# Second layer of an AdaLN/FFN kernel: the e4m3 rounding without its masking step, a shorter scale chain, and the last expert tile's w2 split moved ahead

## The chip, the cores and the metric

The kernel runs on one core of one Trainium2 chip. The time is the device time of one execution in microseconds (us). The engines are TensorE (PE, its weight loads PEld), VectorE (DVE), ScalarE (ACT), GpSimd (POOL) and SyncE (SP). All times on a timeline are us from the start of the profiled span.

## The reference

The input x is 4 x 256 x 256. Two layers follow, each `x = x + ffn(cond(x))`.

- `cond` is a bidirectional recurrence over the 256 rows: forward and backward decaying sums of exp(k) and exp(k)*v, their ratio, times sigmoid(x).
- Layer 1's `ffn` is an attention block (16 heads, 4 key heads) and then a mixture of 8 experts, top 2 of 8 for each row: `silu(h @ w1[e]) * (h @ w3[e]) @ w2[e]`, 256 to 896 to 256 wide.
- Layer 2's `ffn` is quantised. Rows are scaled by their largest absolute value over 448 and rounded to e4m3 (three bits of mantissa), the weights likewise:

```
def _reorder_quantize_x(x, idx):
    scale = jnp.max(jnp.abs(x)) / GLOBAL_DIV
    xr = (x / scale)[:, idx]
    scale_x = jnp.max(jnp.abs(xr), axis=1, keepdims=True) / FP8_MAX
    qx = _fp8(xr / scale_x)
    return (qx, scale_x, scale)
...
g = _qlinear(qx, sx, sc, w_gate, up_reorder_index, out_idx=down_reorder_index)
u = _qlinear(qx, sx, sc, w_up, up_reorder_index, out_idx=down_reorder_index)
t = jax.nn.silu(g) * u
qt, st, sct = _reorder_quantize_x(t, down_reorder_index)
y = _qlinear(qt, st, sct, w_down, down_reorder_index)
```

The inner width is 704.

## The kernel before, in words

The kernel is written engine by engine; each engine has its own list of instructions in a fixed order, and semaphores order them against one another. `link(ins)` lets DVE wait until `ins` has finished before the next instruction may start; without it short instructions overlap in the pipeline.

**The expert loop** (PE L653, ACT L998, DVE L1547). The 1024 rows, each for two experts, are sorted by expert into 23 tiles of 128 rows (MT = 23, tiles 0 to 22). Products with large weights are made with a value split into a high and a low float16 part. For tile n:

- PE makes the up products in two parts (`up`, 512 and 384 columns of w1 and w3), then, one tile behind, the down product (`down`, L635), which waits for the low parts of inner rows and w2 (`inner_low`, `w2lo_done`) and until ACT has copied the output before from the same bank (`y_copied`).
- ACT, in this order: Silu of the first part (L1007), a copy of the next tile's transposed rows, `w2_high` (L971: the high part of the expert's w2, 1792 columns, which waits until the down product of tile n-2 has read the buffer), `inner_high` of the first part, Silu of the second part (L1019), `inner_high` of the second part, the copy of tile n-1's output out of PSUM (L1028) and its write to memory (L1030).
- DVE: `silu(n, 0)` (multiplies the first part, L1519), a piece of side work for layer 2, `silu(n, 1)`, `inner_low(n, 0)` (L1533), `w2_low` (L1526), `inner_low(n, 1)`, another piece of side work.
- At the end of the loop come two folds, in which layer 2's gate and up weights, already multiplied by their scales on POOL, are split into high and low parts: `fold_high` on ACT (L994, behind tiles 20 and 21, since n runs one ahead of the output) and `fold_low` on DVE (L1545, behind tiles 21 and 22).

**Between the layers.** When all outputs are in memory, POOL gathers the two expert outputs of each row (L1846), in five groups of 1, 1, 2, 2 and 2 of the eight 128-row tiles (`GROUPS`). PE waits for the first combined group and then runs fillers (`keep_clock`, L404, products of zeros).

**The second layer**, per group g and tile i:

- DVE `combine` (L1571) adds the two weighted outputs to the residual; ACT takes the Sigmoid (`input_gate`, L1039); DVE `mix_input` multiplies by the ratio (L1595) and calls `scale_of_rows`: the peak of each row (L1579), the output scale peak/448 (L1580), its reciprocal (L1581), and that times 2^20 (L1582). ACT `scaled_input` makes two scaled copies: the value (L1055) and the value times 2^20 (L1056).
- DVE `round_input` calls `nearest_e4m3`: L1586 keeps the exponent bits of the raised copy and sets one bit of the mantissa, which gives the constant 1.5 times a power of two; L1587 adds it (or a least value) to the scaled value, which rounds it; L1588 subtracts it again.
- PE transposes, makes the gate and up products (L686). ACT takes the Silu of the gate (`gate_of_tile`, L1066). DVE `inner_rows` multiplies by the up product (L1614) and calls `scale_of_rows`. ACT `scaled_inner` makes the two copies (L1073, L1074), DVE `round_inner` rounds, PE transposes (L710), ACT copies (L1080), PE makes the down product (L720), DVE `output_rows` scales it (L1631), POOL adds the residual (L1852) and SP writes it.
- DVE's order is written out by hand (L1634 to L1663). In the steady part it is inner_rows(i), round_inner(i-1), output_rows(i-3). ACT's is scaled_inner(j+1), gate_of_tile(j+2), copy_qxT(j+3), copy_qtT(j) (L1107). Before tile 2 ACT loads the table of Silu by a one-column Silu (L1097), behind the Sigmoids of the last groups.

The rounding as it stands:

```
link(V.tensor_scalar(g.bitcast(I32), raised.bitcast(I32), 0x7F800000, 0x00400000, ALU.bitwise_and, ALU.bitwise_or))
link(V.scalar_tensor_tensor(v, g, FP8_LEAST * MAGIC, v, ALU.max, ALU.add))
return V.scalar_tensor_tensor(dst, g, FP8_LEAST * MAGIC, v, ALU.max, ALU.subtract, reverse1=True)
```

Of the kernel before, what the change touches and what calls it, by code (L numbers as in the profile page):

```python
# [7 lines left out]
I32 = mybir.dt.int32  # L8
U32 = mybir.dt.uint32
ALU = mybir.AluOpType  # L10
# [33 lines left out]
FP8_LEAST = 2.0 ** -6  # L44
GROUPS = ((0, 1), (1, 1), (2, 2), (4, 2), (6, 2))
# [20 lines left out]
def build(nc, t, out):  # L66
    ctx = ExitStack()
    with ctx:
# [86 lines left out]
        xval, xraised, xgrid = (cut(breg, 2 * NT * D + k * 2 * D, 2 * D).rearrange("p (i n) -> p i n", i=2) for k in range(3))  # L155

        gate0, gate1, tval0, tval1, tsc0, tsc1, tra0, tra1, tgrid = (cut(areg, 8832 + k * INTER, INTER) for k in range(9))
# [602 lines left out]
        def _(act):  # L760
# [237 lines left out]
            for n in range(MT + 1):  # L998
# [14 lines left out]
                if n < MT:  # L1013
                    w2_high(n, parity)
                    inner_high(n, parity, 0)
                    act.wait_ge(s["upb_done"], n + 1)
# [3 lines left out]
                    if n + SLOTS_UP < MT:  # L1020
                        load_up(act, n + SLOTS_UP)
                    inner_high(n, parity, 1)
# [8 lines left out]
                if n in (20, 21):  # L1031
                    fold_high(n - 20)
# [14 lines left out]
            def scaled_input(g):  # L1047
# [5 lines left out]
                for k in range(count):  # L1053
                    i = first + k
                    nc.scalar.activation(xval[:, k, :], xmix[:, i, :], ACT.Copy, scale=rs[:, 4, i:i + 1])  # L1055
                    last = nc.scalar.activation(xraised[:, k, :], xmix[:, i, :], ACT.Copy, scale=rs[:, 5, i:i + 1])  # L1056
# [12 lines left out]
            def scaled_inner(i):  # L1069
# [4 lines left out]
                nc.scalar.activation(traised[i % 2], tvals[i % 2], ACT.Copy, scale=rs[:, 9, i:i + 1]).then_inc(s["scaled_ready"], 1)  # L1074
# [43 lines left out]
        def _(dve):  # L1118
# [428 lines left out]
            for n in range(MT):  # L1547
# [5 lines left out]
                w2_low(n, n % 2)  # L1553
# [3 lines left out]
                if n >= MT - 2:  # L1557
                    fold_low(n - MT + 2)
# [17 lines left out]
            def scale_of_rows(at, value, i, n, done):  # L1576

                peak, out, inverse, raised = (rs[:, k, i:i + n] for k in at)
                link(V.tensor_reduce(out=peak, in_=value, axis=AX.X, op=ALU.max, apply_absolute_value=True))  # L1579
                link(V.tensor_scalar(out, peak, 1.0 / FP8_MAX, None, ALU.mult))  # L1580
                link(V.reciprocal(inverse, out))  # L1581
                V.tensor_scalar(raised, inverse, 2.0 ** 20, None, ALU.mult).then_inc(done, 1)  # L1582

            def nearest_e4m3(dst, v, raised, g):

                link(V.tensor_scalar(g.bitcast(I32), raised.bitcast(I32), 0x7F800000, 0x00400000, ALU.bitwise_and, ALU.bitwise_or))  # L1586
                link(V.scalar_tensor_tensor(v, g, FP8_LEAST * MAGIC, v, ALU.max, ALU.add))  # L1587
# [291 lines left out]
```

## Time and profile before

| | |
|---|---|
| median of 3 runs | 626.72 us (625.84 to 627.07) |
| the profiled execution | 625.02 us, span 623.2 us |
| mean granted TensorE clock | 0.961 |
| busy: PE, PEld, DVE, ACT, POOL | 495.9, 406.4, 506.2, 361.1, 241.2 us |
| stages | to about 20: loading; to 170 and 310: recurrence, attention; to 540: experts; from 545.8 to 617: second layer |

A timeline row reads: start, duration, engine, line, operation, what is written from what with partitions x elements, how many, and in brackets the idle time before it and what ended it. "issue" there is time in which the engine waited for nothing that the profile shows. The clock is a share of 2.4 GHz; it has two levels, 1.00 and 0.50 (1.2 GHz).

### The profile page before, as it was taken

The page shows a single profiled execution, that of the slowest core. Times are in us where ns is not written, and L with a number is a line of the kernel's source. Part 1 is how long each engine was busy: PE and PEld are TensorE (multiplying, and loading weights), DVE is VectorE, ACT ScalarE, POOL GpSimd, SP SyncE. Part 2 cuts the span into 40 slices and gives each one's busy share as a digit, 9 for nine tenths or more (in the row PEclk, how much of TensorE's full clock was granted, in tenths as well). Part 3 has the DMA queues.
Part 4 walks back from the last instruction along what each step waited for, and adds up shares of the span by engine and source line. Part 5 has one row for each costly group of instructions (what it writes and reads, how often), then busy time and mean ns, then how long its engine had stood idle before and what let it go on. Part 6 is the DMA issues. An engine that isn't in the chain of part 4 may idle for free.

```text
span 623.2 us, 10889 instructions
## 1 busy us (share of the span) xinstructions
PE 495.9 (80%) x3862; PEld 406.4 (65%) x3862; DVE 506.2 (81%) x981; ACT 361.1 (58%) x762; POOL 241.2 (39%) x204
## 2 busy tenths in 40 slices
PE   2011298599999999999748999999999999475774
PEld 1000143278888878888618999999999999332542
DVE  4999878688888888987354979989999899489993
ACT  3336235777787778876307457565555556356671
POOL 3244014744444445541436079642514420170011
PEclk9999999989999999999859999999999999888897
DMA  8300004050000000000149799889888753130001
GB/s 267 135 1 1 0 1 135 0 178 2 1 2 2 1 2 9 19 9 2 58 157 357 259 331 281 273 267 257 300 290 271 274 130 119 34 103 17 9 25 36
DMA packets 36530, 71.87 MB, mean 115 GB/s; under 512 B 5275, under 2 KB 21915, under 8 KB 36219
## 3 DMA queue, kind: packets, MB, share of 16 engines
q10 hardware_dynamic: 15280, 40.77, 19.6%
q1 hardware_dynamic: 18123, 22.26, 10.6%
q0 software_dynamic: 3072, 8.14, 5.2%
q8 instruction: 31, 0.51, 0.4%
q14 instruction: 24, 0.20, 0.1%
HBM read 66.03 MB, written 5.12 MB: 114 GB/s over the span
## 4 chain that ended last, share of the span: by engine, by line
PE 55%; DVE 27%; issue 7%; ACT 5%; DMA 3%; POOL 1%; SPq 1%; DVEq 0%; ACTq 0%; POOLq 0%; PEldq 0%
PE pw L437 9%; PE pb L437 9%; PE pt L631 6%; PE pb L631 6%; PE sc L478 6%; PE sc L631 6%; PE po L437 5%; PE pt L489 3%; DVE areg L1181 2%; DVE areg L1167 2%; DVE areg L1165 2%; DVE rs L1579 2%; DMA wreg<-in_L_ffn_w 1%; DVE breg L1238 1%; DVE areg L1614 1%
## 5 line engine op out<-in xcount | busy, mean ns | idle before, releaser
L1730 POOL TENSOR_TENSOR breg<-breg,con 128x512 f32<-128x512 f32 x32 | 40.7, 1272 | 81.4 <-ACT breg L864 81.4
L437 PE MATMUL pb<-areg,wreg 128*128 128x512 f16 x240 | 58.4, 379 | 2.1 <-ACT breg L864 1.9
L437 PE MATMUL pw<-areg 128*128 128x256 f16 x406 | 56.5, 273 | 2.7 <-DVE areg L1533 2.7
L872 ACT ACTIVATE breg<-breg,mx 128x128 f32<-128x128 f32 (+1 forms) x128 | 56.5, 444 | 2.0 <-DVE mx L1289 2.0
L478 PE MATMUL sc<-areg,breg 128*128 128x128 f32 (+1 forms) x256 | 48.6, 334 | 6.7 <-DVE mx L1289 5.5
L631 PE MATMUL pb<-areg,wreg 128*128 128x128 f32 x448 | 52.7, 275 | 0.6 <-ACT areg L965 0.6
L985 ACT CAST areg<-areg 128x512 f16<-128x512 f32 (+1 forms) x46 | 25.9, 563 | 46.8 <-DVE areg L1519 43.6
L631 PEld LDWEIGHTS pb<-areg,wreg 128*128 128x128 f32 x448 | 51.3, 192 | 0.9 <-issue 0.8
L631 PE MATMUL pt<-areg,wreg 128*128 128x128 f32 x424 | 49.9, 275 | 1.3 <-DMA wreg<-in_L_ffn_w 1.3
L631 PEld LDWEIGHTS pt<-areg,wreg 128*128 128x128 f32 x424 | 48.5, 192 | 1.5 <-DMA wreg<-in_L_ffn_w 1.4
L631 PE MATMUL sc<-areg,wreg 128*128 128x128 f32 x416 | 48.9, 275 | 0.0
L478 PEld LDWEIGHTS sc<-areg,breg 128*128 128x128 f32 x256 | 38.7, 193 | 14.3 <-issue 4.6
L631 PEld LDWEIGHTS sc<-areg,wreg 128*128 128x128 f32 x416 | 47.6, 192 | 0.1
L1725 POOL TENSOR_TENSOR breg<-breg 128x512 f32<-128x512 f32 x32 | 44.5, 1390 | 4.5
L1772 POOL DMA_INDIRECT areg<-h_dram,row_ids x23 | 28.1, 1222 | 45.3 <-PE po L618 33.2
L881 ACT CAST breg<-pt 128x768 f16<-128x768 f32 x32 | 25.5, 798 | 34.4 <-PE pt L489 34.3
L437 PEld LDWEIGHTS pw<-areg 128*128 128x128 f16 x406 | 39.5, 98 | 7.3 <-DVE areg L1533 3.0
L977 ACT ACTIVATE areg<-wreg 128x1792 f16 x23 | 39.2, 1704 | 3.0 <-issue 2.7
L1289 DVE CUSTOM_DVE_ANT_0 breg<-sc,con 128x128 f32<-128x128 f32 (+1 forms) x128 | 38.0, 353 | 2.4 <-PE pt L489 1.6
L437 PEld LDWEIGHTS pb<-areg,wreg 128*128 128x128 f16 x240 | 22.3, 98 | 26.3 <-ACT breg L864 3.4
L1238 DVE TENSOR_TENSOR breg<-pb,con 128x512 f32<-128x512 f32 x40 | 27.5, 687 | 13.4 <-PE pb L437 10.9
L414 PE MATMUL sc<-con,areg 128*128 128x128 f32 x16 | 4.5, 434 | 42.3 <-DVE areg L1184 42.3
(250 smaller groups left out, 1286.4 us busy)
## 6 DMA issues: line engine op xcount, KB each, us to landing
wreg<-in_L_ffn_w ACTq DMA_DIRECT2D x40, 896.0 KB, 8.1
wreg<-in_L_ffn_w SPq DMA_DIRECT2D x14, 896.0 KB, 8.3
ys_dram<-areg ACTq DMA_DIRECT2D x23, 128.0 KB
wreg<-in_L_ffn_wq SPq DMA_DIRECT2D x1, 2048.0 KB, 8.9
wreg<-in_L_ffn_wo SPq DMA_DIRECT2D x1, 2048.0 KB, 8.2
areg<-in_fside_BxSxS ACTq DMA_DIRECT2D x4, 256.0 KB, 5.4
x_in<-in_x SPq DMA_DIRECT2D x4, 256.0 KB, 3.9
h_dram<-areg SPq DMA_DIRECT2D x8, 128.0 KB, 1.7
```

The lines of the kernel that those rows point to most:

```text
L437: last = nc.tensor.matmul(bank, w(a), m(b), start=first and k == 0, stop=final and k == 2)
L478: last = nc.tensor.matmul(sc2[:, b, o:o + w], qr[:, buf, b * S + qb * P:b * S + (qb + 1) * P], kT[:, kv, pair * PAIR + b * S:pair * PAIR + ...
L631: last = nc.tensor.matmul(bank[:, j * P:(j + 1) * P], up_w[n % SLOTS_UP][:, m, c, at:at + P], xsT[:, parity, c * P:(c + 1) * P], start=c = ...
L872: last = nc.scalar.activation(pr[:, parity, b, o:o + w], pr[:, parity, b, o:o + w], ACT.Exp, bias=mx[:, parity, k:k + 1], scale=-1.0, accu ...
L881: nc.scalar.copy(pT[:, parity, 0], pt2[:, :, 0:BLK]).then_inc(s["pThi_done"], 1)
L977: nc.scalar.activation(w2s[parity][0].rearrange("p c n -> p (c n)"), wreg[:, bass.ds((e % RING) * WDOWN, WDOWN)], ACT.Copy, scale=WS).then ...
L985: nc.scalar.copy(hhT[parity][:, 0, lo // P:hi // P, :], inner[:, lo:hi].rearrange("p (c n) -> p c n", n=P))\
L1238: V.tensor_tensor(t1[:, parity, :].rearrange("p (b n) -> p b n", b=2), bank[:, :].rearrange("p (b n) -> p b n", b=2), rope_cos.rearrange(" ...
L1289: last = V.tensor_tensor_reduce(out=pr[:, parity, b, o:o + w], in0=sc2[:, b, o:o + w], in1=mask[:, o:o + w], scale=-SCALE, scalar=3e38, op ...
L1725: G.tensor_tensor(dst, t1[:, parity, :], t2[:, parity, :], ALU.add).then_inc(s["radd_done"], 1)
L1730: G.tensor_tensor(t2[:, parity, :].rearrange("p (b n) -> p b n", b=2), t2[:, parity, :].rearrange("p (b n) -> p b n", b=2), rope_sin.rearr ...
L1772: G.indirect_dma_start(out=xs[n % 4], out_offset=None, in_=h2_dram[:, :], in_offset=bass.IndirectOffsetOnAxis(ap=row_ids[:, n:n + 1], axis ...
```

## The change

- `nearest_e4m3` loses its first instruction. ACT makes the raised value with Abs instead of Copy, and the row's factor becomes 448/peak times (2^20 - 2^10) instead of times 2^20. This value itself, not 1.5 times a power of two, is added and subtracted.
- `scale_of_rows` takes the reciprocal of the peak first (a linked step); the inverse, the raised inverse and the output scale then follow without a link between them. For the input groups the output scale, which was an instruction of its own in `mix_input`, becomes the last of these four.
- The last tile's `w2_high` and `w2_low` go ahead, behind the work of tile 21; on the last tile ACT takes `inner_high` of the first part behind the second Silu. The two `fold_high` move one tile later (the second behind the last output), both `fold_low` behind the last tile.

```diff
+RAISE = 2.0 ** 20 - 2.0 ** 10
...
-                if n < MT:
+                if n < MT - 1:
                     w2_high(n, parity)
                     inner_high(n, parity, 0)
+                if n < MT:
                     act.wait_ge(s["upb_done"], n + 1)
                     if n >= 1:
                         act.wait_ge(s["inner_low"], 2 * n)
                     nc.scalar.activation(inner[:, FA:FF], up_pair(n, 1)[:, 0, 0:FB], ACT.Silu).then_inc(s["silu_b_done"], 1)
                     if n + SLOTS_UP < MT:
                         load_up(act, n + SLOTS_UP)
+                    if n == MT - 1:
+                        inner_high(n, parity, 0)
                     inner_high(n, parity, 1)
...
-                if n in (20, 21):
-                    fold_high(n - 20)
+                if n == MT - 2:
+                    w2_high(MT - 1, 1 - parity)
+                if n >= MT - 1:
+                    fold_high(n - MT + 1)
...
-                    last = nc.scalar.activation(xraised[:, k, :], xmix[:, i, :], ACT.Copy, scale=rs[:, 5, i:i + 1])
+                    last = nc.scalar.activation(xraised[:, k, :], xmix[:, i, :], ACT.Abs, scale=rs[:, 5, i:i + 1])
...
-                nc.scalar.activation(traised[i % 2], tvals[i % 2], ACT.Copy, scale=rs[:, 9, i:i + 1]).then_inc(s["scaled_ready"], 1)
+                nc.scalar.activation(traised[i % 2], tvals[i % 2], ACT.Abs, scale=rs[:, 9, i:i + 1]).then_inc(s["scaled_ready"], 1)
...
-                w2_low(n, n % 2)
+                if n < MT - 1:
+                    w2_low(n, n % 2)
                 inner_low(n, n % 2, 1)
                 if n in beside_b:
                     beside_b[n]()
-                if n >= MT - 2:
-                    fold_low(n - MT + 2)
+                if n == MT - 2:
+                    w2_low(MT - 1, (MT - 1) % 2)
+            for m in range(2):
+                fold_low(m)
...
-            def scale_of_rows(at, value, i, n, done):
+            def scale_of_rows(at, value, i, n, done, step):
 
-                peak, out, inverse, raised = (rs[:, k, i:i + n] for k in at)
+                peak, turned, out, inverse, raised = (rs[:, k, i:i + n] for k in at)
                 link(V.tensor_reduce(out=peak, in_=value, axis=AX.X, op=ALU.max, apply_absolute_value=True))
-                link(V.tensor_scalar(out, peak, 1.0 / FP8_MAX, None, ALU.mult))
-                link(V.reciprocal(inverse, out))
-                V.tensor_scalar(raised, inverse, 2.0 ** 20, None, ALU.mult).then_inc(done, 1)
+                link(V.reciprocal(turned, peak))
+                V.tensor_scalar(inverse, turned, FP8_MAX, None, ALU.mult)
+                V.tensor_scalar(raised, turned, FP8_MAX * RAISE, None, ALU.mult).then_inc(done, 1)
+                return V.tensor_scalar(out, peak, step, None, ALU.mult)
 
-            def nearest_e4m3(dst, v, raised, g):
+            def nearest_e4m3(dst, v, raised):
 
-                link(V.tensor_scalar(g.bitcast(I32), raised.bitcast(I32), 0x7F800000, 0x00400000, ALU.bitwise_and, ALU.bitwise_or))
-                link(V.scalar_tensor_tensor(v, g, FP8_LEAST * MAGIC, v, ALU.max, ALU.add))
-                return V.scalar_tensor_tensor(dst, g, FP8_LEAST * MAGIC, v, ALU.max, ALU.subtract, reverse1=True)
+                link(V.scalar_tensor_tensor(v, raised, FP8_LEAST * MAGIC, v, ALU.max, ALU.add))
+                return V.scalar_tensor_tensor(dst, raised, FP8_LEAST * MAGIC, v, ALU.max, ALU.subtract, reverse1=True)
...
-                scale_of_rows((2, 0, 4, 5), value, first, count, s["xinv_ready"])
-                V.tensor_scalar(rs[:, 3, first:first + count], rs[:, 0, first:first + count], 1.0 / WS, None, ALU.mult).then_inc(s["xout_ready"], 1)
+                scale_of_rows((2, 0, 3, 4, 5), value, first, count, s["xinv_ready"], 1.0 / (FP8_MAX * WS)).then_inc(s["xout_ready"], 1)
...
-                scale_of_rows((6, 7, 8, 9), tval, i, 1, s["inv_ready"])
+                scale_of_rows((6, 1, 7, 8, 9), tval, i, 1, s["inv_ready"], 1.0 / FP8_MAX)
```

The buffers of the masked value (`xgrid`, `tgrid`) are dropped with it.

## Rows read from the trace of the kernel before

**Rows 1.** DVE's timeline, tail of the expert loop: start, us, engine, line, operation.
```profile
529.37 1.62 DVE L1545 SCALAR_TENSOR_TENSOR x_in<-breg,x_in 128x1408 f16<-128x1408 f32 x1
530.91 0.69 DVE L1519 TENSOR_TENSOR areg<-areg,pt 128x512 f32<-128x512 f32 x1
...
533.74 2.02 DVE L1526 SCALAR_TENSOR_TENSOR areg<-wreg,areg 128x1792 f16<-128x1792 f16 x1
535.68 0.55 DVE L1533 TENSOR_TENSOR areg<-areg 128x384 f16<-128x384 f32 x1
...
545.78 1.01 DVE L1571 SCALAR_TENSOR_TENSOR x<-areg,rt,x 128x256 f32<-128x256 f32 x2 [8.01 <-DMA areg<-ys_dram,sloti]
```

**Rows 2.** PE's timeline, the same stretch.
```profile
528.22 2.84 PE L631 MATMUL pb<-areg,wreg 128*128 128x128 f32 x24
...
536.28 2.47 PE L437 MATMUL pw<-areg 128*128 128x256 f16 x21 [2.71 <-DVE areg L1533]
```

**Rows 3.** ACT's timeline, the same stretch.
```profile
527.31 0.33 ACTq L1030 DMA_DIRECT2D ys_dram<-areg  x1
527.69 1.38 ACT L994 ACTIVATE w_up<-breg 128x1408 f16<-128x1408 f32 x1 [0.41 <-ACT areg L1028]
...
529.70 1.71 ACT L977 ACTIVATE areg<-wreg 128x1792 f16 x1
...
533.94 0.39 ACT L1028 ACTIVATE areg<-pw 128x256 f32<-128x256 f32 x1
```

**Rows 4.** Busy time and granted clock in windows: PE, PEld, DVE, ACT, POOL, PEclk, DMA.
```profile
589.00:609.00 20.00, 14.15 (x113) 9.55 (x110) 19.18 (x37) 13.01 (x17) 2.19 (x3) 1.00 0.07 23
...
571.80:575.20 3.40, 3.40 (x14) 1.80 (x12) 2.85 (x8) 0.85 (x1) 0.00 (x0) 0.50 0.00 0
```

**Rows 5.** DVE's timeline, second layer, tiles 2 and 5.
```profile
575.68 0.95 DVE L1614 SCALAR_TENSOR_TENSOR areg<-pb,rs,areg 128x704 f32<-128x704 f32 x1 [0.86 <-issue]
...
594.13 0.94 DVE L1614 SCALAR_TENSOR_TENSOR areg<-pb,rs,areg 128x704 f32<-128x704 f32 x1
...
596.02 0.15 DVE L1580 TENSOR_SCALAR rs<-rs 128x1 f32<-128x1 f32 x1
...
596.49 0.53 DVE L1586 TENSOR_SCALAR areg<-areg 128x704 int32<-128x704 int32 x1
597.05 0.89 DVE L1587 SCALAR_TENSOR_TENSOR areg<-areg 128x704 f32<-128x704 f32 x1
...
599.18 0.94 DVE L1614 SCALAR_TENSOR_TENSOR areg<-pb,rs,areg 128x704 f32<-128x704 f32 x1
```

**Rows 6.** DVE's groups of line 1586 by shape: busy us, mean ns, idle before.
```profile
L1586 DVE TENSOR_SCALAR areg<-areg 128x704 int32<-128x704 int32 x8 | 4.3, 533 | 0.6 <-PE pt L710 0.6
...
L1586 DVE TENSOR_SCALAR breg<-breg 128x512 int32<-128x512 int32 x3 | 1.3, 418 | 0.0
...
L1586 DVE TENSOR_SCALAR breg<-breg 128x256 int32<-128x256 int32 x2 | 0.6, 294 | 0.9 <-ACT breg L1056 0.9
```

**Rows 7.** ACT's timeline, second layer, ahead of tile 2 and at tile 5.
```profile
569.42 1.28 ACT L1097 ACT_TABLE_LOAD   x1
...
596.60 0.88 ACT L1073 ACTIVATE areg<-areg,rs 128x704 f32<-128x704 f32 x1 [1.04 <-DVE rs L1582]
...
598.16 0.83 ACT L1066 ACTIVATE areg<-sc,rs 128x704 f32<-128x704 f32 x1
```

**Rows 8.** PE's timeline, second layer: products of tile 2, of tile 7, and the tail.
```profile
571.34 2.11 PE L686 MATMUL sc<-x_in,areg 128*128 128x352 f16 x8 [0.46 <-ACT areg L1045]
573.24 2.34 PE L686 MATMUL pb<-w_up,areg 128*128 128x352 f16 x8
...
601.91 1.36 PE L686 MATMUL pb<-w_up,areg 128*128 128x352 f16 x8
...
609.04 0.82 PE L710 MATMUL pt<-identb,areg 128*88 128x128 f16 x8 [3.10 <-DVE areg L1588]
609.65 1.92 PE L720 MATMUL pw<-areg 88*128 88x256 f16 x8
```

More of the change, by code:

```diff
@@ L154, in build @@
         xsig, xmix = (cut(breg, k * NT * D, NT * D).rearrange("p (i n) -> p i n", i=NT) for k in range(2))
-        xval, xraised, xgrid = (cut(breg, 2 * NT * D + k * 2 * D, 2 * D).rearrange("p (i n) -> p i n", i=2) for k in range(3))
-        gate0, gate1, tval0, tval1, tsc0, tsc1, tra0, tra1, tgrid = (cut(areg, 8832 + k * INTER, INTER) for k in range(9))
+        xval, xraised = (cut(breg, 2 * NT * D + k * 2 * D, 2 * D).rearrange("p (i n) -> p i n", i=2) for k in range(2))
+        gate0, gate1, tval0, tval1, tsc0, tsc1, tra0, tra1 = (cut(areg, 8832 + k * INTER, INTER) for k in range(8))
         tscaled, traised = (tsc0, tsc1), (tra0, tra1)
@@ L1603, in round_input @@
                     dve.wait_ge(s["qxT_done"], first + count - 4)
-                nearest_e4m3(qx[:, first // 2 % 2, first % 2:first % 2 + count, :], xval[:, 0:count, :], xraised[:, 0:count, :],
-                             xgrid[:, 0:count, :]).then_inc(s["qx_ready"], 1)
+                nearest_e4m3(qx[:, first // 2 % 2, first % 2:first % 2 + count, :], xval[:, 0:count, :], xraised[:, 0:count, :]).then_inc(s["qx_ready"], 1)
             def inner_rows(i):
@@ L1623, in round_inner @@
                     dve.wait_ge(s["qtT_done"], i)
-                nearest_e4m3(qt[:, :], tscaled[i % 2], traised[i % 2], tgrid).then_inc(s["qt_ready"], 1)
+                nearest_e4m3(qt[:, :], tscaled[i % 2], traised[i % 2]).then_inc(s["qt_ready"], 1)
             def output_rows(i):
```

## The prediction

> **What bounds the kernel now.** I read the busy time by stage first, then for the two stretches that the change touches the timelines of VectorE (DVE), ScalarE (ACT) and TensorE (PE), then the groups of DVE instructions. Two stretches matter.
>
> The tail of the expert loop. On tile 22, the last, DVE multiplies the first half at 530.91 and must then wait for ACT's second Silu before it can multiply the second; behind that come the low split of w2 at 533.74, which holds the engine for two us, and the low half of the inner rows at 535.68 [rows 1]. PE had finished the last up products at 531.06 (528.22 + 2.84) and starts the last down product at 536.28, after 2.71 us of waiting for that last DVE instruction [rows 2]. ACT is no better: after the first Silu of tile 22 it makes the high w2 split (529.70, 1.71 us), so that its second Silu comes late, though its input was there at 531.06 [rows 2, 3]. Everything after the last down product is a chain of a copy, a write, a gather and then DVE at 545.78 [rows 1]; DVE idles 8 us for it, so a us gained at 536.28 is a us of the end.
>
> The second layer, from 545.8 on. In the stretch of tiles 5 to 7 DVE is busy 19.18 of 20 us, PE 14.15, ACT 13.01 [rows 4]. A tile takes DVE 5.05 us (594.13 to 599.18) [rows 5].
>
> **The change, part by part.**
>
> (1) The tail. Removed from tile 22: ACT's w2 split between the two Silus and DVE's low split between the two low halves. They go behind tile 21, in the place of one fold. The steps after:
> - ACT: the write of tile 20 is issued at 527.31 and takes 0.33; then the register load and the split of 1.71, from about 527.97 to 529.67. It replaces the fold of 1.38 there (527.69), so the first Silu of tile 22 starts 0.6 later, at about 529.55 [rows 3]. This costs nothing: DVE comes to it later still.
> - DVE: the low split (two us) takes the place of the fold of 1.62 at 529.37; it waits for ACT and runs 529.72 to 531.65, so the first multiplication of tile 22 goes from 530.91 to 531.65.
> - ACT's second Silu starts at 531.10 (PE's 531.06), ends 531.6. DVE's second multiplication follows at 532.25, the two high halves on ACT at 532.3 and 532.8, the low halves on DVE at 532.9 and 533.5, ending 534.05.
> - The last down product also waits until ACT has copied the output of tile 21 out of the same bank: 533.94 + 0.39 = 534.33 [rows 3]. That ends last: start 534.38. Gain 536.28 - 534.38 = 1.90 us.
> - The folds. ACT issues a write, folds (1.38) from 534.74 to 536.1, copies tile 22 at 536.9, and folds again 537.7 to 539.1; DVE's two folds of 1.62 end at 537.8 and 540.8. The gather brings DVE's next work at 545.78 - 1.90 = 543.88, so 3.1 us of cover is left. Without it the second fold would cost its 1.62. The table load behind the second fold ends before 540.5, under the same cover. The queues of SP and POOL get nothing new and nothing of theirs is passed; the write of tile 22 is issued before the second fold.
>
> (2) The masking instruction on line 1586 goes: eight of 704 columns, three of 512, two of 256 [rows 6]. From start to start they hold DVE 0.56 (596.49 to 597.05 [rows 5]) for 704 columns; for the others I add the 0.03 of hand-over that this shows over the mean: 0.45 and 0.32. Sum 4.48 + 1.35 + 0.64 = 6.5 us of DVE.
>
> (3) The scale chain. Before, three short instructions, two of them linked: 596.02 to 596.49, 0.47 [rows 5], which I split as two linked steps of 0.20 and a last one of 0.07. After, one linked step and three of 0.07, 0.41: 0.06 falls. For the five input groups, where the output scale was a fourth instruction already (0.54), 0.13 falls. ACT's scale is ready 0.13 earlier: one linked step of 0.20 less, one of 0.07 more. So 8 x 0.06 + 5 x 0.13 = 1.1 us of DVE.
>
> (4) Abs for Copy on ACT: no row has Abs. The nearest rows are Copy with the scale (0.88) and Silu with the scale, as wide (0.83): I take 0.88, no change; with 0.83 each tile would gain 0.05. The other end is a table load in front of it, 1.28; that is a rival below [rows 7]. The two Copies and the Silus and Sigmoids alternate already with no load for Copy, which is why I stay at the near end.
>
> What of (2) and (3) reaches the end? Not all, and this is where I chose. Times are of the trace before, without the 1.90.
> - To the first instruction of tile 2 (575.68 [rows 5]) DVE loses 0.64 + 0.45 + 2 x 0.56 and 4 x 0.13 + 2 x 0.06, together 2.85, and it had waited 0.86 there: it would be ready at 571.97. But it waits for PE's up products, which end at 575.58 (573.24 + 2.34), and these stand behind a table load on ACT (569.42), which follows the last combine [rows 7, 8]. Up to that combine only 0.64 + 0.56 + 3 x 0.13 + 2 x 0.06 = 1.71 falls, some 0.05 of it taken back by PE at tile 1. So tile 2 is 1.66 earlier.
> - From there to tile 4 two of 512, one of 704, 0.13 and 2 x 0.06 go: 1.71. Together 3.37. ACT's gate of tile 5, behind its scaling of tile 3 and the four instructions of the last input group, comes 0.14 later than that: 3.23.
> - Tiles 5, 6, 7. By DVE alone a tile would go from 5.05 to 5.05 - 0.56 - 0.06 = 4.43. But there is a second ring: a tile's first DVE instruction, peak, scale, then on ACT in order Copy, raised value and the Silu of the gate, which the next tile's first DVE instruction waits for. Before: 594.13 to 596.60 is 2.47, to 598.16 another 1.56 [rows 5, 7], the Silu 0.83, ending 598.99, and DVE goes on at 599.18: only 0.19 of slack. After: 2.34 + 1.56 + 0.83 + 0.06 of hand-over = 4.79. So each of three tiles gains 0.26, not 0.62: 0.78. Sum 4.01.
> - The last period's 0.56 + 0.06 on DVE counts in full, 4.63 in all, up to PE's transposes before 609.65. From there PE is in front: its down product takes 1.92 at the lower clock where eight larger ones took 1.36 at the upper [rows 8], and fillers follow. The last masking instruction is hidden there.
>
> Sum: 1.90 + 4.63 = 6.5 us. The profiled execution took 625.02 us (span 623.2), so 618.5 by its own time; it was 1.7 under the median of the runs shown, 626.72, and I forecast against the median: 620.2 us.
>
> The Trainium skill (ScalarE: Activation LUTs, "Table sets: the hidden batching unit") says that abs, like relu and copy, is in every table set. By that the rival with table loads doesn't exist and the sum is the same; the same page ("What ACT_TABLE_LOAD costs") gives about 2.66 us for a switch with its drain, where the trace's loads take 1.28 each [rows 7]. No run here has yet shown Abs.
>
> **The rivals.**
> - PE keeps its upper clock. At 571.8 to 575.2 it was granted 0.50 of full speed, 1.2 instead of 2.4 GHz; at 589 to 609 it was 1.00 [rows 4]. The eight products of 1.92 at 609.65 are at the lower level too, and 3.10 us without work lie before 609.04 [rows 8]. With a faster DVE these gaps get shorter (about 2.5 and 2.85 us by the sums above). If the first fall goes, two lots of products take 2.6 (twice 1.36 with a little overlap) instead of 4.24 (573.24 + 2.34 - 571.34 [rows 8]) and tile 2 comes 1.7 earlier, as DVE is ready; if the second goes too, the last masking instruction counts, 0.6. Time 618.5 with the first alone, 617.9 with both. Against it: the fall isn't tied to the gap alone, and ACT still paces some of it. Chance 0.22.
> - The ring over ACT doesn't bind (another order of arrival than I read). Then 3 x 0.36 = 1.1 more: 619.1. For it: my slack of 0.19 is a small difference of large times. Chance 0.08.
> - The tail gains nothing: something else holds tile 22, say the high halves on ACT, or the two late folds meet the gather. Against it is the 3.1 us of cover. Time 626.72 - 4.63 = 622.1. Chance 0.12.
> - The change does not do what it says: DVE's busy time falls, but waits for PE and ACT take its place entirely. DVE's 19.18 of 20 us speaks against. 626.7, chance 0.04.
> - Slower: Abs isn't in the loaded table. Then each tile of the second layer has a load before Abs and one before the next Silu, in the ring: 2 x 1.28 = 2.56 per tile, eight tiles 20.5, less 6.5: 640.7. It decides from three such tiles on (7.7 against 6.5). Chance 0.03.
>
> **How the numbers follow.** Forecast as summed: 0.51. The predicted time is that case's, 620.2. Downward the range takes in the clock (617.9) and 0.5 for the spread of the runs of before (625.84 to 627.07): 617.4. Upward it takes in the tail without gain and the same spread: 622.6. Left out are the last two rivals and unforeseen ones. Faster by over 0.2% (1.25 us, about what a measurement of this kernel can tell from no change): 0.93; within: 0.04; slower: 0.03.
>
> **What would show it.** The last down product some 1.9 us earlier, and PE's wait before it under 1 us; no line 1586; between tiles 5 and 6 4.8 us, with DVE waiting about 0.4 for ACT's Silu; no more table loads than before; the same clock falls, or fewer. The forecast is wrong if the period is 4.4, if DVE's first combine still comes at 545.8, or if Abs is longer than 0.88.

## The result

| | runs | median | lowest to highest | profiled execution (span) |
|---|---|---|---|---|
| before | 4 | 626.89 us | 625.84 to 629.23 | 625.02 (623.2) |
| changed | 4 | 619.79 us | 616.89 to 623.62 | 616.89 (615.0) |
| changed, measured once more | 6 | 620.15 us | 619.24 to 623.46 | 619.38 (617.5) |

Changed over before is 0.9893 (95% interval 0.9851 to 0.9935), and 0.9895 (0.9869 to 0.9920) the second time: faster by about 1%. That is 7.1 us by the medians of the table and 6.6 us by the second ratio (the runs of before beside the second measurement had a median of 628.34, which is 8.2 us more than its 620.15). The forecast was 620.2, in a range of 617.4 to 622.6. Three executions of before in the later comparisons took 1828 us; they are in a slow state and left out of every ratio. The runs of the changed kernel spread over 6.7 us, those of before over 3.4.

The profiled execution of the changed kernel is the fastest of its runs, 8.1 us under that of before. Three stretches make this up. 0.8 us is gained before the expert tail begins, in work that the change doesn't touch (the last w2 split but one starts at 526.17 on DVE, at 526.97 before); it belongs to the execution, not to the change. From there to DVE's first combine 0.5 us (18.32 against 18.81), from the first combine to DVE's last output scaling 6.94 (63.91 against 70.85). The rest behind it is equal (6.60, 6.57).

**The profile after.** Line numbers are those of the changed kernel. DVE's timeline in the tail of the expert loop (for [rows 1]; columns: start, us, engine, line, operation, idle before):

```profile
526.17 2.02 DVE L1532 SCALAR_TENSOR_TENSOR breg<-wreg,areg 128x1792 f16<-128x1792 f16 x1
...
529.59 2.02 DVE L1532 SCALAR_TENSOR_TENSOR areg<-wreg,areg 128x1792 f16<-128x1792 f16 x1 [0.94 <-ACT areg L978]
531.54 0.68 DVE L1525 TENSOR_TENSOR areg<-areg,pt 128x512 f32<-128x512 f32 x1
532.13 0.54 DVE L1525 TENSOR_TENSOR areg<-areg,pb 128x384 f32<-128x384 f32 x1
532.90 1.16 DVE L1539 TENSOR_TENSOR areg<-areg 128x512 f16<-128x512 f32 x2 [0.22 <-ACT areg L986]
...
538.81 1.63 DVE L1551 SCALAR_TENSOR_TENSOR w_up<-breg,w_up 128x1408 f16<-128x1408 f32 x1 [1.53 <-ACT w_up L995]
544.49 1.00 DVE L1580 SCALAR_TENSOR_TENSOR x<-areg,rt,x 128x256 f32<-128x256 f32 x2 [4.05 <-DMA areg<-ys_dram,sloti]
```

The split of tile 22 now stands ahead of both multiplications, and waits 0.94 for ACT. ACT's timeline, the same stretch (for [rows 3]):

```profile
526.51 0.33 ACTq L1034 DMA_DIRECT2D ys_dram<-areg  x1
527.69 1.70 ACT L978 ACTIVATE areg<-wreg 128x1792 f16 x1 [1.21 <-issue]
...
533.45 0.38 ACT L1032 ACTIVATE areg<-pw 128x256 f32<-128x256 f32 x1
```

PE's timeline, the last down product (for [rows 2]):

```profile
534.12 2.46 PE L438 MATMUL pw<-areg 128*128 128x256 f16 x21 [1.34 <-DVE areg L1539]
```

POOL's timeline behind the last write, in the changed kernel:

```profile
539.47 1.85 POOL L1853 DMA_INDIRECT areg<-ys_dram,sloti  x1 [27.00 <-DMA ys_dram<-areg]
541.62 0.97 POOL L1853 DMA_INDIRECT areg<-ys_dram,sloti  x1 [0.30 <-issue]
```

The same in the kernel before:

```profile
541.63 1.01 POOL L1846 DMA_INDIRECT areg<-ys_dram,sloti  x1 [29.02 <-DMA ys_dram<-areg]
542.95 0.97 POOL L1846 DMA_INDIRECT areg<-ys_dram,sloti  x1 [0.30 <-issue]
```

The first gather takes 1.85 us in place of 1.01, and begins while DVE makes its second fold (538.81 to 540.44).

DVE's timeline in the steady part of the second layer (for [rows 5]):

```profile
587.66 0.95 DVE L1621 SCALAR_TENSOR_TENSOR areg<-pb,rs,areg 128x704 f32<-128x704 f32 x1 [0.28 <-ACT areg L1072]
...
589.57 0.16 DVE L1589 RECIPROCAL rs<-rs 128x1 f32<-128x1 f32 x1
589.76 0.15 DVE L1590 TENSOR_SCALAR rs<-rs 128x1 f32<-128x1 f32 x1
...
589.96 0.88 DVE L1596 SCALAR_TENSOR_TENSOR areg<-areg 128x704 f32<-128x704 f32 x1
...
592.43 0.95 DVE L1621 SCALAR_TENSOR_TENSOR areg<-pb,rs,areg 128x704 f32<-128x704 f32 x1 [0.28 <-ACT areg L1072]
```

ACT's timeline, the same tile (for [rows 7]):

```profile
590.01 0.88 ACT L1079 ACTIVATE areg<-areg,rs 128x704 f32<-128x704 f32 x1 [1.22 <-DVE rs L1591]
590.80 0.87 ACT L1080 ACTIVATE areg<-areg,rs 128x704 f32<-128x704 f32 x1
591.57 0.83 ACT L1072 ACTIVATE areg<-sc,rs 128x704 f32<-128x704 f32 x1
```

A tile takes 4.77 us (587.66 to 592.43). DVE, which never waited here before, now waits 0.28 for ACT's Silu (L1072): the releaser in the bracket names the ring. Abs (L1080) takes 0.87 as Copy did. PE's timeline at tile 2 and at the end (for [rows 8]):

```profile
561.38 5.30 PE L405 MATMUL pt<-zeros 128*128 128x512 f16 x16
567.50 0.28 PE L679 MATMUL po<-identb,areg 128*128 128x128 f16 x2 [0.82 <-DVE areg L1597]
568.61 1.37 PE L687 MATMUL sc<-x_in,areg 128*128 128x352 f16 x8 [0.82 <-ACT areg L1051]
569.81 1.36 PE L687 MATMUL pb<-w_up,areg 128*128 128x352 f16 x8
...
601.37 0.64 PE L711 MATMUL pt<-identb,areg 128*88 128x128 f16 x8 [2.82 <-DVE areg L1597]
601.85 1.03 PE L721 MATMUL pw<-areg 88*128 88x256 f16 x8
```

The fillers ahead of tile 2 and the wait behind them, in the kernel before:

```profile
563.87 3.62 PE L404 MATMUL pt<-zeros 128*128 128x512 f16 x16
570.59 0.28 PE L678 MATMUL po<-identb,areg 128*128 128x128 f16 x2 [3.10 <-DVE areg L1588]
```

The products that took 2.11, 2.34 and 1.92 us, for the most part at 1.2 GHz, take 1.37, 1.36 and 1.03: here they ran at the upper level. But PE did not stay there all the time. Its 16 fillers ahead of tile 2 took 5.30 us in place of 3.62, with a granted clock of 0.66 from 561 to 566 us, so the fall of the clock came earlier and lay in work that nothing waits for. It also left PE idle for 0.82 us and not 3.10 ahead of tile 2. Windows of the same trace (columns as in [rows 4]):

```profile
561.00:566.00 5.00, 5.00 (x22) 2.19 (x23) 4.82 (x14) 3.98 (x7) 0.00 (x0) 0.66 0.09 26
567.00:572.00 5.00, 3.21 (x22) 2.00 (x23) 4.62 (x10) 3.07 (x7) 0.00 (x0) 1.00 0.00 0
...
601.30:608.00 6.70, 5.20 (x46) 3.65 (x47) 3.32 (x6) 2.02 (x2) 2.17 (x3) 1.00 0.13 43
```

### The profile page after: what moved, and what is told of

Its sections match the earlier page's. It is cut to its first block, busy times and chain, and to the rows that moved or that the text cites. A ratio compares the mean times of both kernels' runs of the same rounds, so it can differ in the third digit from the quotient of the medians.

```text
span 615.0 us, 10884 instructions
## 1 busy us (share of the span) xinstructions
PE 492.3 (80%) x3862; PEld 403.7 (66%) x3862; DVE 500.0 (81%) x976; ACT 360.6 (59%) x762; POOL 242.3 (39%) x204
## 4 chain that ended last, share of the span: by engine, by line
PE 55%; DVE 26%; issue 6%; ACT 5%; DMA 3%; POOL 1%; SPq 1%; ACTq 0%; DVEq 0%; POOLq 0%; PEldq 0%
PE pw L438 10%; PE pb L438 9%; PE pt L632 6%; PE pb L632 6%; PE sc L479 6%; PE sc L632 6%; PE po L438 5%; PE pt L490 3%; DVE areg L1187 2%; DVE areg L1173 2%; DVE areg L1171 2%; DVE rs L1588 1%; DVE areg L1532 1%; DMA wreg<-in_L_ffn_w 1%; DVE areg L1621 1%
```

## The experiments

Every kernel was timed beside runs of before; "over before" is the ratio with its interval. This was done in three sets, in which before had medians of 626.62 us (tail alone, ACT turned, mask and chain back), 626.35 (rounding alone, folds, register load, 22 fillers) and 628.34 (the last three), so a difference of medians from different sets can hold up to 2 us that no edit made. Since single executions differ by several us, the stages of the traces decide, and the medians say whether it shows in the end. A table of the stages, worked out from the DVE, PE and POOL timelines, stands behind the experiments.

### Tail of the expert loop alone

The edit: the kernel before with the diff's hunks on `w2_high`, `w2_low`, `inner_high`, `fold_high` and `fold_low`, and nothing else of it.

> The kernel before with the tail of the expert loop changed alone. The prediction: the last down product 1.9 us earlier and the end 1.9 us earlier. Theory now: the w2 split behind the write of tile 20 starts 1.2 us after ACT's last work, not 0.66, so the down product gains 1.4, and the late second fold on DVE stretches POOL's first gather from 1.0 to 1.85, so DVE's first combine gains about 0.5 and the whole 0.5. Rival: the 1.85 was chance, then the gain is 1.4.

Measured: 626.64 us, over before 0.9990 (0.9971 to 1.0010). The last down product starts 7.95 us behind the w2 split of tile 21, as in the changed kernel (before: 9.31), so it gained 1.36; the first gather takes 1.87; from that split to the first combine it is 18.38 us (before 18.81). The tail edit alone brings 0.4 us, which the medians can't tell from nothing. The rival, that 1.85 was chance, falls: the gather is long in all eight profiles with the late folds.

### Rounding and scale chain alone

The edit: the changed kernel with those hunks undone.

> The changed kernel with the tail of the expert loop as before: rounding and scale chain alone. Theory: nearly the whole gain is here: second layer as in the changed kernel (periods 4.77), first combine 9.5 us behind the last down product as before; 4.6 us faster than before where PE's clock falls ahead of tile 2 and in the tail, up to 6.9 where it doesn't, so 1 to 1.5 per cent between them. Rival (the tail brings 1.9 us): only 4.6 us of the 7.1 are here, and this is 1.9 us behind the changed kernel.

Measured: 621.33 us, over before 0.9919 (0.9889 to 0.9949), so 5.0 us of the 7 by medians. Its periods are 4.77 us. In its trace the last down product ran largely at the lower clock (granted 0.50 from 537 to 539 us):

```profile
537.08 3.98 PE pw L438 x21
```

(chain of waits; start, us, what). 3.98 us where 2.46 to 2.48 is usual, so here the first combine came 11.07 us behind the start of that product. I hadn't expected this. Before it PE waits 2.7 us in the order of before [rows 2] and 1.34 in the changed one. Of three profiles with the old order two show the fall (the other is the kernel before with 23 fillers, 3.84 us), of ten with the new order none. So the tail edit may be worth more in the medians (here 621.33 against 619.79 and 620.15) than the 0.4 us of the traces at equal clock. That isn't shown: the three intervals overlap. By the median alone, 5.0 us is nearer to the rival's 4.6 than to "nearly the whole gain"; the stages of the traces, with 0.4 us for the tail, are what speaks against the rival's 1.9.

### ACT's order turned in the steady part

```diff
             for j in range(2, NT):
-                if j + 1 < NT:
-                    scaled_inner(j + 1)
                 if j + 2 < NT:
                     gate_of_tile(j + 2)
+                if j + 1 < NT:
+                    scaled_inner(j + 1)
```

> The changed kernel with ACT's order in the steady part turned: the gate's Silu of tile j+2 ahead of the scaling of tile j+1. Theory (a ring DVE product, peak, scale, ACT scaling twice, Silu, next DVE product sets the period of tiles 4 to 7): the ring is cut, the period falls from 4.77 to about 4.42, DVE's own work, DVE's 0.28 us wait for the Silu goes, and the kernel is about 1.0 us faster than the changed one. Rival (DVE with its hand-overs, or PE, sets 4.77): period and time stay.

Measured: 619.39 us, over before 0.9877 (0.9847 to 0.9906). DVE's products of tiles 4 to 6:

```profile
586.22 0.95 DVE L1621 SCALAR_TENSOR_TENSOR areg<-pb,rs,areg 128x704 f32<-128x704 f32 x1
590.63 0.94 DVE L1621 SCALAR_TENSOR_TENSOR areg<-pb,rs,areg 128x704 f32<-128x704 f32 x1
595.04 0.94 DVE L1621 SCALAR_TENSOR_TENSOR areg<-pb,rs,areg 128x704 f32<-128x704 f32 x1
```

Period 4.41 and no bracket: DVE waits for nothing (tile 7's product follows at 599.45, 4.41 later again). With the ring cut, DVE's own work (forecast 4.43) is the bound. The median moved by 0.4 to 0.8 of the 1.0 expected, within the spread; the trace itself had the lower clock at tile 2.

### The mask put back

```diff
+                link(V.tensor_scalar(raised.bitcast(I32), raised.bitcast(I32), 0x7F800000, 0x00400000, ALU.bitwise_and, ALU.bitwise_or))
                 link(V.scalar_tensor_tensor(v, raised, FP8_LEAST * MAGIC, v, ALU.max, ALU.add))
```

(and RAISE = 2^20).

> The changed kernel with the masking instruction put back (in place, on the raised value). Theory: DVE's work is then 4.42 + 0.56 = 4.98 per tile, over the ring's 4.77, so the period is 4.98, and the eight, three and two instructions cost about 3.5 us up to tile 4, 0.6 over tiles 5 to 7 and 0.6 behind: 4.5 us slower than the changed kernel with the same clock. Rival (other engines wait anyway, the mask was hidden): under 1.5 us slower.

Measured: 624.73 us, over before 0.9965 (0.9950 to 0.9979): 4.6 to 4.9 us behind the changed kernel by medians and 4.4 to 4.5 by ratios, where 4.5 was expected. The periods are 4.98, 4.97, 4.96, and in tiles 5 to 7 DVE waits for nothing. The mask is most of the gain.

### The old scale chain put back

```diff
-                link(V.reciprocal(turned, peak))
-                V.tensor_scalar(inverse, turned, FP8_MAX, None, ALU.mult)
-                V.tensor_scalar(raised, turned, FP8_MAX * RAISE, None, ALU.mult).then_inc(done, 1)
-                return V.tensor_scalar(out, peak, step, None, ALU.mult)
+                link(V.tensor_scalar(turned, peak, 1.0 / FP8_MAX, None, ALU.mult))
+                link(V.reciprocal(inverse, turned))
+                last = V.tensor_scalar(raised, inverse, RAISE, None, ALU.mult)
```

(and the output scale behind it for the input groups alone.)

> The changed kernel with the scale chain of before (three short instructions in a row, then the output scale), still without the mask. Theory: the scale reaches ACT 0.13 later, which the ring passes on in full: period 4.90, and 0.13 for each input group besides, 1.2 to 1.4 us slower in all. Rival (DVE's own work is the bound): DVE has 0.28 of slack per tile, so the period stays at 4.77 and the cost is under 0.7.

Measured: 620.64 us, over before 0.9901 (0.9872 to 0.9930). DVE's products of tiles 5 and 6:

```profile
593.86 0.95 DVE L1622 SCALAR_TENSOR_TENSOR areg<-pb,rs,areg 128x704 f32<-128x704 f32 x1 [0.32 <-ACT areg L1072]
598.76 0.95 DVE L1622 SCALAR_TENSOR_TENSOR areg<-pb,rs,areg 128x704 f32<-128x704 f32 x1 [0.31 <-ACT areg L1072]
```

Period 4.90. DVE had slack, so its 0.06 more would have been hidden; the 0.13 by which ACT gets its scale later is passed on whole. Together with the mask this shows the ring from both sides: 0.56 more of DVE cost 0.20 per tile (4.77 to 4.97), 0.13 more in the ring cost 0.13. The total (0.5 to 0.9 by medians, 1.2 to 1.4 expected) is within the spread.

### The folds early

```diff
                     if n == MT - 1:
+                        fold_high(0)
                         inner_high(n, parity, 0)
...
-                if n >= MT - 1:
-                    fold_high(n - MT + 1)
+                if n == MT - 1:
+                    fold_high(1)
```

> The changed kernel with ACT's first fold put behind the second Silu of tile 22, where ACT is idle 1.46 us, and the second in the first's place; DVE then folds twice right behind the last low half. Theory (the late second fold on DVE, which overlaps POOL's first gather, stretches that gather from 1.0 to 1.85): the gather takes 1.0, the first combine comes 9.5 us behind the last down product and not 10.4, 0.85 us faster. Rival (1.85 comes from something else, the shorter time between write and gather say): it stays at 1.85.

Measured: 620.01 us, over before 0.9891 (0.9865 to 0.9917). The first gather in POOL's timeline:

```profile
539.45 1.01 POOL L1854 DMA_INDIRECT areg<-ys_dram,sloti  x1 [27.44 <-DMA ys_dram<-areg]
```

DVE's two folds in the same trace:

```profile
533.96 1.62 DVE L1552 SCALAR_TENSOR_TENSOR x_in<-breg,x_in 128x1408 f16<-128x1408 f32 x1
535.63 1.63 DVE L1552 SCALAR_TENSOR_TENSOR w_up<-breg,w_up 128x1408 f16<-128x1408 f32 x1
```

With the folds over at 537.3 the gather takes 1.01 again, and the first combine comes 9.58 us behind the start of the last down product (changed 10.37, before 9.50). So the late second fold is what stretched it, and the write-to-gather time is not. In the median 0.8 us is not to be seen. In the changed kernel the gather starts 0.66 behind the fold's start and ends 0.88 behind its end (541.32 against 540.44), nearly its own 1.01: as if it stood still under the fold. The Trainium skill (SBUF — State Buffer, "SBUF: two separate sides") calls the port pair that VectorE and GpSimd share an exclusive lock, held for a whole instruction by whichever starts first, VectorE's with two SBUF inputs among them if GpSimd's reads SBUF; the traces agree, with 1.85 against 1.01. One more thing changes with the edit: ACT's table load starts within 0.03 us of DVE's second fold in all eight profiles, and is gone from there too. Alone it doesn't fit as the cause: in the changed kernel it lies over the gather for 0.61 us (to 540.08), less than the 0.84 by which the gather is longer, while the fold lies over it for 0.97. No run separates the two.

### The register load ahead

```diff
+                if n == MT - 2:
+                    last_e = act.value_load(tmi[0:1, bass.ds(MT - 1, 1)], min_val=0, max_val=NE - 1)
+                    act.wait_ge(s["w_ready"], last_e + 1)
                 if n >= 1:
                     act.wait_ge(s["down_done"], n + 1)
...
-                    w2_high(MT - 1, 1 - parity)
+                    w2_high(MT - 1, 1 - parity, last_e)
```

> The changed kernel with ACT's register load for the w2 split of tile 22 ahead of its wait for the down product of tile 20, so ahead of the write. Theory (the load of the register behind the write, 1.2 us before the split, is what missed in the forecast of 1.90): the split starts 0.5 to 0.8 us earlier and the last down product 0.5 earlier. Rival (the split was not what ended last): the down product stays 6.1 us behind the w2 split of tile 20's successor and nothing moves.

Measured: 619.14 us, over before 0.9885 (0.9856 to 0.9915). ACT's timeline:

```profile
526.65 0.39 ACT L1036 ACTIVATE areg<-pw 128x256 f32<-128x256 f32 x1 [0.19 <-issue]
527.07 0.33 ACTq L1038 DMA_DIRECT2D ys_dram<-areg  x1
527.58 1.70 ACT L979 ACTIVATE areg<-wreg 128x1792 f16 x1 [0.54 <-ACT areg L1036]
```

The wait ahead of the split is 0.54 in place of 1.21; 0.19 of it now stands ahead of the copy. The last down product starts 7.56 us behind tile 21's split on DVE, not 7.95: 0.39 earlier, where 0.5 was expected. ACT's split starts 1.14 us behind DVE's split of tile 21 (527.58 against 526.44) and not 1.52 (527.69 against 526.17): 0.38 earlier, less than the 0.5 to 0.8 of the theory. The edit moves the register load together with the wait for the weights (`w_ready`) that follows it; which of the two costs the time, no run tells.

### Twenty-two fillers ahead of tile 2

```diff
-            keep_clock(pt2[:, 1, :], 16)
+            keep_clock(pt2[:, 1, :], 22)
```

> The changed kernel with 22 fillers of PE for 16 ahead of tile 2. Theory (PE's clock ahead of tile 2 is what spreads the runs of the changed kernel: 26.8 us from the first combine to tile 2's product on DVE at the upper clock, about 29 at the lower): with PE idle for under 1.5 us there, the fall in tile 2's products goes, 27 us in every profile, and the median of the runs comes down by 0.5 to 1.5 us. Rival (the fall isn't bound to that gap): the spread stays and the median too.

Measured: 619.00 us, over before 0.9880 (0.9857 to 0.9903), and the six runs lie between 618.14 and 620.87: 2.7 us, where the changed kernel's ten lie over 6.7. Tile 2 comes 26.77 us behind the first combine, as in both profiles of the changed kernel. The median is 0.8 to 1.2 lower, but the intervals overlap: no gain is shown. Nor does its trace bear out the theory that the fall goes (the second line is a window, with the columns of [rows 4]; 0.50 is its granted clock):

```profile
562.68 6.60 PE L405 MATMUL pt<-zeros 128*128 128x512 f16 x22
564.00:565.00 1.00, 1.00 (x4) 0.36 (x3) 0.96 (x4) 1.00 (x3) 0.00 (x0) 0.50 0.00 0
```

At the pace of before (16 in 3.62 us) 22 fillers would take 5.0 us, and they took 6.60: the fall is there, among the fillers. It is in all 13 profiles, once ahead of or in tile 2's products. In six of the ten with 16 fillers (before, tail alone, rounding alone, ACT turned, chain back, load ahead) the fillers took 3.62, PE was idle for 2.50 to 3.10 us, and the products met the lower level. In the other four (changed, changed again, folds early, mask back) the fillers took 4.60 to 5.30, PE was idle for 0.82 to 1.59, and the products ran at the upper level. The three profiles with 22 or 23 fillers are like these four. Whether more fillers bring the fall forward, or it would have come there anyway, three profiles against four of ten can't tell.

### The kernel before with 23 fillers

The same edit on the kernel before, 23 for 16.

> The kernel before with 23 fillers for 16 ahead of tile 2 and nothing else. Theory (the gap of 3.1 us ahead of tile 2 is what lets PE's clock fall): its second layer comes to tile 2's product 1.5 us earlier (28.3 instead of 29.9 us from the first combine) and the median falls by 1 to 1.5 us. Rival (clock falls are not to be had by the gap's length): no change in either.

Measured: 627.30 us, over before 0.9999 (0.9976 to 1.0022): a miss. In its trace the products of tile 2, from 574.2 to 576.8, ran at the upper level (granted clock 1.00; 0.50 in [rows 4]), the fall lay in the fillers ahead of them (23 in 6.30 us, 0.50 from 568 to 569), and tile 2's product on DVE came 16.13 us behind tile 1's in place of 17.07, 0.9 less and not 1.5. But tile 0 had met the lower level (11.81 us from the first combine, before 10.34), its last down product had met it too (3.84 us), and nothing is left in the median. Taking away one place for a fall doesn't pay where the others stay.

### The changed kernel once more

No edit.

> The changed kernel once more, to see what its own profile owes to the clock. Theory: another profile shows the same first combine (10.4 behind the last down product), the same periods (4.77), but in two of three cases tile 2 about 29 us behind the first combine in place of 26.8, and a median near 619.8. Rival (the 26.8 belongs to the change itself): 26.8 again and all runs near 617.

Measured: 620.15 us, over before 0.9895 (0.9869 to 0.9920). First combine 10.34 behind, periods 4.76 to 4.78, and again 26.78 to tile 2: the likely case of my theory did not come. The fall lay at the end instead:

```profile
603.16 1.22 PE L405 MATMUL pt<-zeros 128*128 128x512 f16 x3
605.16 1.87 PE L721 MATMUL pw<-areg 88*128 88x256 f16 x8 [0.78 <-DVE areg L1638]
606.82 1.06 PE L711 MATMUL pt<-identb,areg 128*88 128x128 f16 x8
607.67 1.91 PE L405 MATMUL pt<-zeros 128*128 128x512 f16 x4
```

From the first combine to DVE's last output 65.98 us, against 63.91 in the first profile, all of the 2.07 behind tile 7. Two profiles of one kernel with equal orders differ by 2 us through where the clock falls.

### All four edits together

ACT's order, the register load, the folds, and 22 fillers.

> The changed kernel with the four edits together: ACT's steady order turned, the register load ahead, the folds early, 22 fillers. Theory: they are worth 1.0 (period 4.41 in place of 4.77, three tiles), 0.4 (w2 split of tile 22), 0.85 (first gather 1.0 instead of 1.85) and the clock's share of about 1; the pieces stand one behind another, so they add: 2 us under the changed kernel in traces with the same clock, and a median of 616.5 to 617.5. Rival: PE, with fillers longer and tiles shorter, becomes the bound (a tile takes it 4.26) or falls in the tail, and less than 1 us is left.

Measured: 615.18 us in five runs (614.91 to 617.23), over before 0.9805 (0.9783 to 0.9826). It beats both kernels: its interval lies clear of the changed kernel's, and its median 5.0 us under that of the changed kernel measured beside it. That is more than the 3.3 expected, and 615.18 is below the 616.5 to 617.5 of the theory: the sum of the pieces missed on this side. The periods are 4.40 to 4.41, the first gather 1.01, the first combine 9.51 behind, the last output 62.96 behind the first combine. Fastest run against fastest run it is 614.91 to 616.89, the 2.0 of the sum for equal clocks; the other 3 us of the medians would then be clock falls that it no longer meets. That share is argued from the runs' spread; only one trace of it was seen. The traces name one place for it. Ahead of the transposes of the last tile PE is idle for 2.45 us in the two profiles with ACT's order turned, and neither met the lower level there. In the six with 2.82 us four did (rounding alone, folds early, load ahead, changed again), in the five with 2.95 to 3.10 all.

**Ahead of the stages.** Up to tile 21's w2 split on DVE no edit touches anything, and yet the 13 profiles come to it between 526.15 us (folds early) and 529.64 (chain back). These 3.5 us are half of the spread of the changed kernel's runs, so that spread isn't made by the clock at tile 2 alone.

**The stages**, in us. Columns: from tile 21's w2 split on DVE to the last down product; to the first combine; first gather; first combine to tile 2's product; period; first combine to last output.

| | to down | to combine | gather | tile 2 | period | last output |
|---|---|---|---|---|---|---|
| before | 9.31 | 18.81 | 1.01 | 29.90 | 5.05 | 70.85 |
| changed | 7.95 | 18.32 | 1.85 | 26.78 | 4.77 | 63.91 |
| tail alone | 7.95 | 18.38 | 1.87 | 30.27 | 5.06 | 71.21 |
| rounding alone | 9.31 | 20.38 | 1.01 | 29.24 | 4.77 | 66.96 |
| ACT turned | 7.94 | 18.31 | 1.87 | 29.25 | 4.41 | 65.48 |
| mask back | 7.94 | 18.40 | 1.86 | 28.35 | 4.97 | 70.41 |
| chain back | 7.94 | 18.40 | 1.85 | 28.90 | 4.90 | 68.69 |
| folds early | 7.95 | 17.53 | 1.01 | 26.93 | 4.77 | 64.59 |
| load ahead | 7.56 | 18.00 | 1.86 | 28.43 | 4.77 | 66.08 |
| 22 fillers | 7.94 | 18.31 | 1.86 | 26.77 | 4.77 | 63.90 |
| changed again | 7.95 | 18.29 | 1.86 | 26.78 | 4.77 | 65.98 |
| before, 23 fillers | 9.31 | 20.23 | 1.01 | 30.72 | 5.06 | 73.11 |
| all four | 7.64 | 17.15 | 1.01 | 26.94 | 4.41 | 62.96 |

## Why the prediction was right, and where it was not

- **The sum.** 6.5 us forecast, 7.1 measured by medians and 6.6 by the second ratio. The direction, the size and the range held; that the total came so near is in part luck. In the traces the tail gave 0.5 of its 1.90. The second layer, for which I forecast 4.63, gave 3.89 (rounding alone), 4.77 (load ahead), 4.87 (changed again), 6.26 (folds early) and 6.94 (changed) against the one profile of before, by where the clock fell. With the middle of these the traces add up to 5.4 us. So the 1.4 us missing from the tail were made up by something that is in no term of my sum. A fall in the last down product, which cost 1.5 us in two of three profiles with the old order, would do it; how often it comes is not shown.
- **(1), the tail: 1.90 forecast, 1.36 at the last down product and 0.5 at the first combine.** Two steps failed. The first is "the register load and the split ... from about 527.97": 0.66 us from the start of the write to the split, where it took 1.18 (526.51 to 527.69). The register load behind the write lay open. The edit that moves it ahead gave 0.39 of the missing 0.54 back; the other 0.15 stays open. So DVE's last low half ended last (534.06), and the copy of tile 21's output, which I had ending last, ended just before it, at 533.83. The second is "the queues of SP and POOL get nothing new" with "3.1 us of cover": the cover against DVE was there (4.05 us of idle before the combine), but the second fold stood beside POOL's gather, and that is on the path. 0.85 us, shown by the folds moved away. I had priced the fold at nothing on DVE's own time, and had not asked what else runs beside it, though my own numbers had the two together: the gather of before starts at 541.63, less 1.90 is 539.73, and the second fold was to end at 540.8.
- **(2), the mask.** Right. Its instructions counted on DVE up to tile 4 (put back, tile 4's product comes 3.54 us later, 41.95 against 38.41 from the first combine), with 0.20 per tile behind it. Put back, it costs 4.4 to 4.9 us in all.
- **(3), the scale chain.** Right in size (0.41 from the reciprocal to the next instruction for a tile: 589.57 to 589.96 is 0.39), and right in where it counts: 0.13 per tile in the ring.
- **(4), Abs.** 0.87, and the table loads are as many as before; this rival is dead. The trace agrees with the rule of the Trainium skill that abs is in every table set (ScalarE: Activation LUTs, "Table sets: the hidden batching unit").
- **The ring.** Forecast 4.79, measured 4.77, with the wait in the profile named after ACT's Silu. Cut, it is 4.41 against the forecast 4.43 of DVE alone. The rival "the ring doesn't bind" is dead. DVE's wait for the Silu was 0.28 where I had named about 0.4 as the sign, and PE's wait ahead of the last down product 1.34 where I had named under 1.
- **Tile 2 and the end.** To tile 4's product I forecast 3.23 gained from the first combine; the first profile has 4.88 (43.29 to 38.41). To the last output, 4.63 forecast, 6.94 in the profile. The differences are 1.65 and 2.31, and the rival with the upper clock had priced them at 1.7 and 2.3. So in its times this execution is the rival's, in both places, and I had given that rival 0.22. Its reason is not the one I gave: PE did not keep its upper clock ahead of tile 2, it fell among the fillers, where that costs nothing. Of the nine profiles with the shorter rounding, four (ACT turned, chain back, rounding alone, load ahead) show tile 2 at 28.4 to 29.3 us and the other five at 26.8 to 26.9; the two profiles of the changed kernel differ at the end instead. Where the fall did hit tile 2's products, as in my sum, tile 4's product gained 2.21 (rounding alone, ACT turned) and 3.04 (load ahead), less than my 3.23: in the first two it covered both lots, 2.53 and 2.56 us, where before had 2.11 and 2.34. I had taken the fall to stay as long as before. Each execution can thus meet the clock's falls in other places, and one chance for one case doesn't describe that.
- **The rival "the tail gains nothing".** Near to the truth in the traces at equal clock, 0.4 to 0.5, and the tail alone measured 0.9990, which 0.4 us and nothing both fit. It named the two late folds meeting the gather as one way, which is what they did, on POOL and not on DVE. Its price, 622.1, is 2.3 over the median; that the difference is the clock's part is argued and not shown.
- **What stays open.** How much the tail edit gains in the medians by sparing the last down product a fall of the clock (two of three profiles against none of ten). How often each place meets a fall; one profile per kernel can't count it. What makes the executions differ by 3.5 us ahead of the changed work.

## What to carry to other kernels

After taking work from the busiest engine, look for the ring of hand-overs through the other engines: here 0.62 us of DVE work (mask and scale chain) was worth 0.28 a tile, until the order of two ScalarE instructions was turned. Work moved into idle time of its own engine is free only if nothing on the path runs beside it on a shared resource; a fold under a gather cost 0.85 us. And where two executions of one kernel differ by 2 us, compare stages and periods first, and medians after. Look at the clock in the fillers too: products at the upper level don't say that the clock never fell.

## What the runs showed of the hardware

- A POOL gather that starts under a DVE instruction with two SBUF inputs takes 1.85 to 1.87 us in place of 1.01, in eight profiles out of eight; in the five without the overlap 1.01.
- ACT's register load and the wait that follows it, behind a write: 1.21 us of idle time before the next ACTIVATE; with both ahead of the write 0.54.
- The granted clock in early, unchanged work differs between executions: in the profile of the four edits together it was 0.61 from 20 to 100 us, in that of the changed kernel once more 1.00 there. The first came to tile 21's w2 split at 528.62, the second at 526.62: 2.0 us, before any of the changed work. The clock isn't shown to be the reason: the two other profiles with 0.61 came to it at 528.61 and 529.64, but that of the mask put back, with 1.00, at 528.82.
- PE fell to its lower level in tile 2's products with 2.50 us without work ahead of them (ACT turned), in the fillers with 2.11 us ahead of the transposes before them (changed), and stayed at the upper with 2.82 (changed, at the end); with the same 2.82 it fell in four other profiles. What a gap costs can't be read from its length alone.
- The same 16 fillers took 3.62 us in six profiles and 4.60 to 5.30 in four. Where they were slow, tile 2's products were fast.
